# Attention and a mixture of experts on one core: a norm in six chunks, beta added during steps 1 to 3, one scan for all experts, scores s5 ahead of sums o0

## The reference

```
xn  = layernorm(x)
qkv = xn @ w_qkv                      # 16 heads of 8
a   = softmax(causal(q k^T / sqrt(8))) v
t1  = layernorm(a @ w_proj + b_proj + xn) * gamma + beta
p   = softmax(xn @ Wr^T)              # 8 experts
t2  = sum over the two largest p[e] of p[e] * (gelu(xn @ W1[e] + b1[e]) @ W2[e] + b2[e])
out = x + t1 + t2
```

## Time and profile before

| | |
|---|---|
| median of 3 runs | 849.73 us (847.44 to 850.27) |
| the profiled execution | 851.77 us, span 850.0 us |
| granted TensorE clock, mean | 0.958 of full speed |
| busy: PE, DVE, ACT, POOL | 699.9, 692.9, 525.4, 536.0 us |
| share of the chain that ended last | PE 56%, DVE 13%, issue 7%, POOL 7%, DMA 6%, ACT 5%, SP's queue 5% |

### The profile page before, as it was taken

The page is one execution under the profiler, slowest core; times in us unless marked ns, Lnnn a source line. Parts: engine busy times, 40 slices in busy tenths (PEclk is TensorE's granted clock), DMA queues, the critical chain, the costliest instruction groups (busy, mean ns, idle before and its releaser), DMA issues.

```text
span 850.0 us, 24989 instructions
## 1 busy us (share of the span) xinstructions
PE 699.9 (82%) x7877; PEld 518.1 (61%) x7878; DVE 692.9 (82%) x1617; ACT 525.4 (62%) x1039; POOL 536.0 (63%) x575
## 2 busy tenths in 40 slices
PE   1366579999999999999888888868999999999800
PEld 1243346666666666666655555537888889888800
DVE  5778878898999998989889999557788888888744
ACT  4541346565656565656556565537989999999800
POOL 8750456767676776767777777334767676667710
PEclk9999899999999999999999999978999999999955
DMA  8294122232323232232233432202222222222189
GB/s 220 80 400 122 64 84 94 81 111 79 114 77 111 80 111 94 94 98 90 84 127 107 139 125 78 64 7 62 84 85 80 85 88 84 82 82 82 56 266 335
DMA packets 113313, 93.66 MB, mean 110 GB/s; under 512 B 16618, under 2 KB 97650, under 8 KB 113268
## 3 DMA queue, kind: packets, MB, share of 16 engines
q1 hardware_dynamic: 95508, 70.26, 27.0%
q0 software_dynamic: 8704, 18.17, 5.9%
q10 hardware_dynamic: 9056, 4.66, 1.9%
HBM read 43.85 MB, written 48.93 MB: 109 GB/s over the span
## 4 chain that ended last, share of the span: by engine, by line
PE 56%; DVE 13%; issue 7%; POOL 7%; DMA 6%; ACT 5%; SPq 5%; DVEq 0%; ACTq 0%; POOLq 0%
PE wide L1259 10%; PE bank_head L1148 7%; PE wide L1113 5%; PE bank_head L1250 5%; PE bank_maxB L1250 5%; PE bank_maxA L1127 4%; PE bank_maxB L1127 3%; DMA xn_rows<-parts_dram 3%; DMA k_cat<-qk_rows 3%; DVE shift L911 3%; POOL probs L581 3%; PE bank_misc L1173 3%; SPq L478 2%; PE bank_maxB L1131 2%; PE bank_maxA L1131 2%
## 5 line engine op out<-in xcount | busy, mean ns | idle before, releaser
L581 POOL TENSOR_SCALAR_AFFINE_SELECT probs<-probs 128x512 f32<-128x512 f32 (+1 forms) x192 | 158.3, 833 | 103.6 <-ACT probs L653 102.8
L653 ACT ACTIVATE probs<-wide 128x1024 f32<-128x1024 f32 x192 | 188.8, 1018 | 47.3 <-PE wide L1117 24.5
L619 POOL DMA_INDIRECT parts_dram<-o_T,dest x144 | 161.0, 1118 | 74.7 <-issue 48.6
L572 POOL DMA_INDIRECT x_slots<-xn_rows,slot_i x128 | 127.3, 995 | 62.8 <-DVE slot_i L868 31.4
L911 DVE TENSOR_REDUCE shift<-bank_maxA 128x2 f32<-128x512 f32 (+1 forms) x192 | 132.1, 688 | 20.1 <-PE bank_maxA L1131 12.9
L911 DVE TENSOR_REDUCE shift<-bank_maxB 128x2 f32<-128x512 f32 (+1 forms) x192 | 131.5, 685 | 4.9 <-PE bank_maxB L1131 0.8
L687 ACT ACTIVATE probs<-wide,b_all 128x256 f32<-128x256 f32 x288 | 121.4, 478 | 16.8 <-PE wide L1259 10.0
L1148 PE MATMUL bank_head<-probs,v_aug 128*32 128x256 f32 (+1 forms) x2048 | 98.9, 334 | 19.1 <-POOL probs L581 18.9
L1259 PE MATMUL wide<-xgT_raw,xnT 128*128 128x256 f16 x864 | 109.2, 277 | 3.7 <-DVE xgT_raw L1020 3.6
L1003 DVE TENSOR_TENSOR probs<-probs 128x512 f16<-128x512 f32 x144 | 99.7, 692 | 5.5 <-ACT probs L693 1.1
L1127 PE MATMUL bank_maxA<-k_cat,q_diag 128*128 128x128 f16 (+1 forms) x512 | 76.2, 252 | 28.5 <-DVE shift L911 19.5
(11 more groups left out here) (174 smaller groups left out, 1252.4 us busy)
## 6 DMA issues: line engine op xcount, KB each, us to landing
qk_rows<-split SPq DMA_DIRECT2D x32, 512.0 KB, 3.2
x_slots<-fill SPq DMA_DIRECT2D x16, 598.5 KB, 7.6
fill<-x_slots SPq DMA_DIRECT2D x72, 133.0 KB
q_diag<-qk_rows SPq DMA_DIRECT2D x256, 32.0 KB
k_cat<-qk_rows SPq DMA_DIRECT2D x64, 128.0 KB
xn_rows<-parts_dram SPq DMA_DIRECT2D x8, 1024.0 KB, 11.8
x_all<-in_x SPq DMA_DIRECT2D x8, 512.0 KB, 7.6
pieces_f<-in_w SPq DMA_DIRECT2D x8, 512.0 KB, 4.8
```

Source lines behind the costliest of these rows:

```text
L572: pool.indirect_dma_start(out=x_slots, out_offset=bass.IndirectOffsetOnAxis(ap=slot_i[:, t, c:c + 1], axis=0), in_=xn_rows[:, t, :], in_of ...
L581: pool.affine_select(out=part, in_=part, compare_op=ALU.is_ge, fill=0.0, base=0, pattern=[[0, n], [1, P]], channel_multiplier=-1).then_inc ...
L619: pool.indirect_dma_start(out=parts_dram, out_offset=bass.IndirectOffsetOnAxis(ap=dest[:, of, t:t + 1].bitcast(U32), axis=0), in_=y[:, of ...
L653: act.activation(probs[:, u, :], ps[:, :], ACT.Exp, scale=SCALE).then_inc(empty, 1)
```

## The change

- The norm's chunks become six, (0,8), (8,16), (16,24), (24,40), (40,56), (56,64); ScalarE normalises 13 groups and VectorE three. VectorE's low parts of step 0 come after the sixth chunk. The memset of q_diag is cut in two, and router and qkv weights have semaphores of their own.
- Beta is added in four parts after the picks (beside step 1), two at the end of step 2 and two at the end of step 3, on GpSimd.
- The counts per tile come ordered by expert, and one scan over 512 elements, with a 0 in a multiplier at each expert's first tile, does the work of eight. The weights leave `places` and are made by `weights` at the end of step 2 on VectorE.
- Sends begin in step 3 (SEND = FINISH). In even steps from 24 the places are m0, m0, s2 instead of m0, s1, s3.
- In `USES`, s5 comes ahead of o0 and shift.
- ScalarE's high part of a weight piece is made behind `v` instead of at the end of the step.

```diff
-        SEND = SOFT
+        SEND = FINISH
...
-            ("wide0", "s4", SOFT), ("maxB", "m11", MAXIMA), ("head", "o0", SOFT),
-            ("misc", "shift", MAXIMA), ("wide1", "s5", SOFT), ("head", "proj", FINISH),
+            ("wide0", "s4", SOFT), ("maxB", "m11", MAXIMA), ("wide1", "s5", SOFT),
+            ("head", "o0", SOFT), ("misc", "shift", MAXIMA), ("head", "proj", FINISH),
...
-                places = ("m0", "s1", "s3") if (s - TAIL) % 2 == 0 else SEND_AFTER
+                places = ("m0", "m0", "s2") if (s - TAIL) % 2 == 0 else SEND_AFTER
...
-        ACT_GROUPS = 12
+        ACT_GROUPS = 13
...
-        MOMENTS = [(0, 8), (8, 16), (16, 32), (32, 48), (48, 64)]
+        MOMENTS = [(0, 8), (8, 16), (16, 24), (24, 40), (40, 56), (56, 64)]
...
-            pool.memset(q_diag[:, 0, :, :, :], 0.0).then_inc(consts, 1)
             for c, (begin, end) in enumerate(MOMENTS):
+                if c < 2:
+                    pool.memset(q_diag[:, 0, 2 * c:2 * c + 2, :, :], 0.0).then_inc(consts, 1)
...
-            for c in range(BETA_PARTS):
+            def add_beta(c):
                 tiles_ = slice(NT // BETA_PARTS * c, NT // BETA_PARTS * (c + 1))
-                wait_normed(pool, 2 * c + 1)
                 pool.tensor_tensor(x_all[:, tiles_, :], x_all[:, tiles_, :],
...
+            pool.wait_ge(route, ROUTE_PICKED + 1)
+            for c in range(BETA_PARTS // 2):
+                add_beta(c)
...
                 if isinstance(s, int) and s == SEND:
                     pool.wait_ge(slots_filled, 256)
-                    pool.wait_ge(route, ROUTE_DONE)
+                    pool.wait_ge(route, ROUTE_WEIGHTS)
...
                     if what == SUM_AFTER and has(s, FINISH):
                         sums(s)
+                if s in (2, 3):
+                    for c in range(2 * s, 2 * s + 2):
+                        add_beta(c)
                 if has(s, FINISH):
...
-            act.wait_ge(weights_loaded, 96)
+            act.wait_ge(qkv_loaded, 16)
...
+                        for i in pieces(s):
+                            high_piece(i)
...
-                for e in range(E):
-                    V.tensor_tensor_scan(place[:, :, e], ones[:, :], total.rearrange("p (t e) -> p t e", e=E)[:, :, e],
-                                         padded[:, e:e + 1], ALU.mult, ALU.add).then_inc(route, 1)
-                    route_count += 1
-                dve.wait_ge(exp_router, 2)
-                then(V.tensor_reduce(red[:, :], prob[:, :, :], axis=AX.X, op=ALU.add))
+                first_tile_total = total.rearrange("p (e t) -> p e t", e=E)[:, :, 0]
+                then(V.tensor_tensor(first_tile_total, first_tile_total, padded[:, :], ALU.add))
+                dve.wait_ge(consts, 31)
+                then(V.tensor_tensor_scan(place_by_expert[:, :, :].rearrange("p e t -> p (e t)"), goes_on[:, :, :].rearrange("p e t -> p (e t)"), total, 0.0,
+                                          ALU.mult, ALU.add))
...
+            def weights():
+
+                nonlocal route_count
+                dve.wait_ge(exp_router, 2)
+                then(V.tensor_reduce(red[:, :], prob[:, :, :], axis=AX.X, op=ALU.add))
+                V.tensor_scalar(xn_rows[:, :, D + 4], best[:, 0, :], -1.0, float(E), ALU.mult, ALU.add).then_inc(route, 1)
+                route_count += 1
+                then(V.reciprocal(xn_rows[:, :, D], red[:, :]))
+                then(V.scalar_tensor_tensor(out=xn_rows[:, :, D + 2], in0=top[:, 1, :], scalar=-1.0, in1=xn_rows[:, :, D],
+                                            op0=ALU.add, op1=ALU.mult))
...
+                if isinstance(s, int) and s == SOFT:
+                    weights()
...
             moments(4)
             low_group(4)
+            low_group(5)
+            tiles_moments(56, 64)
+            offsets(4)
+            moments(5)
+            low_group(6)
+            step(0, 0)
+            low_group(7)
...
-            dve.wait_ge(offset_ready, BETA_PARTS)
```

More of the change, by code:

```diff
@@ L109, in attention_and_moe @@
         piece = (pieces_f32[:, 0, :], pieces_f32[:, 1, :])
-        others, place, rank, prob = (probs[:, u, 0:NT * E].rearrange("p (t e) -> p t e", e=E) for u in range(4))
+        others, place, rank = (probs[:, u, 0:NT * E].rearrange("p (t e) -> p t e", e=E) for u in range(3))
+        place_by_expert = probs[:, 3, 0:NT * E].rearrange("p (e t) -> p e t", e=E)
+        prob = sb("prob", [P, NT, E])
+        goes_on = probs[:, 5, 512:1024].rearrange("p (e t) -> p e t", e=E)
         is_top16, key16 = (probs[:, 4, NT * E // 2 * u:NT * E // 2 * (u + 1)].bitcast(BF16).rearrange("p (t e) -> p t e", e=E) for u in range(2))
@@ L171, in attention_and_moe @@
         x_loaded = [sem(f"x_loaded{c}") for c in range(2 * CHUNKS)]
+        router_loaded = sem("router_loaded")
+        qkv_loaded = sem("qkv_loaded")
         weights_loaded = sem("weights_loaded")
@@ L382, in attention_and_moe @@
         EXPERTS_PACKED = 16
-        ROUTE_DONE = 38
-        MOMENTS = [(0, 8), (8, 16), (16, 32), (32, 48), (48, 64)]
-        assert NT == 64 and 4 * ACT_GROUPS == MOMENTS[-1][0]
+        ROUTE_DONE = 27
+        ROUTE_WEIGHTS = 31
+        MOMENTS = [(0, 8), (8, 16), (16, 24), (24, 40), (40, 56), (56, 64)]
+        assert NT == 64
         EARLY_AFTER = 4
@@ L653, in exp, with high_piece @@
                 act.activation(probs[:, u, :], ps[:, :], ACT.Exp, scale=SCALE).then_inc(empty, 1)
+            def high_piece(i):
+                act.wait_ge(piece_loaded[i % 2], 16 * (i // 2 + 1))
+                act.activation(part_of(i, 0), piece[i % 2], ACT.Copy).then_inc(piece_high, 1)
             def step(s, par):
@@ L678, in step @@
                         exp(s, int(what[1:]))
-                for i in pieces(s):
-                    act.wait_ge(piece_loaded[i % 2], 16 * (i // 2 + 1))
-                    act.activation(part_of(i, 0), piece[i % 2], ACT.Copy).then_inc(piece_high, 1)
             def hidden(s, par, e, half_):
@@ L953, in last @@
                 dve.wait_ge(rstd2_ready, b * 1 + 1)
+                if isinstance(s, int) and s == LAST:
+                    dve.wait_ge(offset_ready, BETA_PARTS)
                 for t in range(QT):
@@ L1034, in _ @@
             moments(1)
-            tiles_moments(16, 24)
+            tiles_moments(16, 20)
             offsets(1)
-            tiles_moments(24, 32)
+            low_router()
+            tiles_moments(20, 24)
             moments(2)
+            tiles_moments(24, 28)
             low_group(0)
+            offsets(2)
+            tiles_moments(28, 32)
+            low_group(1)
             tiles_moments(32, 40)
-            offsets(2)
-            low_group(1)
-            tiles_moments(40, 48)
             moments(3)
             low_group(2)
-            tiles_moments(48, 56)
+            tiles_moments(40, 48)
             offsets(3)
             low_group(3)
-            step(0, 0)
-            tiles_moments(56, 64)
+            tiles_moments(48, 56)
             moments(4)
             low_group(4)
-            dve.wait_ge(rstd_ready, 5)
-            cols = slice(*MOMENTS[4])
-            V.tensor_scalar(mean[:, cols], mean[:, cols], 0.5, None, ALU.mult).then_inc(prep, 1)
-            prep_count += 1
-            dve.wait_ge(prep, prep_count)
+            low_group(5)
[5 more added lines that the diff above has]
+            low_group(7)
+            dve.wait_ge(rstd_ready, 6)
+            half_of_mean(ACT_GROUPS)
             for g in range(ACT_GROUPS, GROUPS):
                 normalise_group(g)
-                low_group(g - ACT_GROUPS + 5)
-            for g in range(GROUPS - ACT_GROUPS + 5, GROUPS):
+                low_group(g - ACT_GROUPS + 8)
+            for g in range(GROUPS - ACT_GROUPS + 8, GROUPS):
                 low_group(g)
             picks()
-            dve.wait_ge(offset_ready, BETA_PARTS)
             steps(dve, step, after=((), (places,)), first_tile=lambda: tile(0, 0, None))
@@ L1096, in count_picks @@
                 pe.wait_ge(route, ROUTE_PICKED + 1)
-                for n_, counting in enumerate((after16, ones16)):
+                for n_, (counting, order_) in enumerate(((after16, "p t e -> p (t e)"), (ones16, "p t e -> p e t"))):
                     for c in range(2):
-                        last = M(wide[1][:, 512 * n_:512 * (n_ + 1)], counting[:, :], pick16[:, c, :, :].rearrange("p t e -> p (t e)"),
+                        last = M(wide[1][:, 512 * n_:512 * (n_ + 1)], counting[:, :], pick16[:, c, :, :].rearrange(order_),
                                  start=(c == 0), stop=(c == 1))
```

42 lines of the change are left out of this document (27 added, 15 removed).

## The result

The changed kernel takes 860.05 us (median of four, 855.81 to 861.56) against 849.25 for the kernel before in the same comparison; the ratio is 1.0129, 95% interval 1.0088 to 1.0169. The prediction was 854.2, range 841 to 860, with "slower" as the likeliest sign: the sign was right, the size was not. The profiled execution took 861.56 us with a span of 859.5, so the spans differ by +9.5 us where the prediction's sum was +4.5.

What follows compares the result with a forecast made beforehand. The attention loop takes most time, bound by dependency cycles with TensorE and VectorE nearly full. Terms -10.8 + 0.45 - 0.7 + 3.8 + 0.45 + 8.6 + 2.7 = +4.5 us on the 849.73 median gave 854.2 us, range 841 to 860.

Steps and rivals of the forecast that it cites:

- The start: Up to o0 of step 2: 10.8 us gained, bound by SyncE's queue, less 0.45 for s5's new place.
- One scan: Places on VectorE: one scan of 512 takes 1.4 us instead of 2.02 for eight; hidden, counted as nothing.
- Step 2 to 3: Beta 4, 5 at step 2's end and no sends there: -0.7 us, s5's price included; from -2 to +2.
- The end of step 3: Beta 6, 7 on GpSimd block VectorE's packing of the experts: +3.8 us; s5's order adds 0.45 to step 4.
- s5 ahead of o0: Attention loop: s5's matmuls delay o0, copy and proj, no new wait: +0.45 us a step, 8.6 over 19 steps.
- rival A: Attention loop: s5's new order is free or gains up to 0.25 us a step; 840.6 or 836 us; chance 0.22.
- Steps 24 on: Late loop steps with sends, transfers and weight pieces: +2.7 us in sum, from -6 to +9.
- order: s5's new order in the late steps: +0.45 us in each of nine steps, 4.1 in all.
- places: Third tile's sends moved earlier in late even steps: -1.2 us in each of three, -0.8 for step 24.
- high parts: Late steps: ScalarE converts a weight piece earlier and waits for its load: 0.5 us in six steps, +3.0.
- The signs to look for: Expected in a later profile: step 14.4 us, no o1 wait, 0.35 at proj, store near 73, packing 8 us long.

Runs made afterwards that it cites:

- run 5: Changed kernel with GpSimd's last two beta parts, at the end of step 3, waiting until VectorE has packed the experts: 858.69 us, ratio 1.0102.
- run 2: Kernel before with one edit only, s5 ahead of o0 and shift in USES: 867.84 us, ratio 1.0201.
- run 7: Kernel before with s5 ahead of o0 and shift, and only half of s3's exponentials made from step 3 on: 866.07 us, ratio 1.0172.
- run 8: Changed kernel with both tiles of a step sent behind m0, none behind the mask of s2: 861.00 us, ratio 1.0129.
- run 3: Changed kernel with GpSimd masking s5 only after all of VectorE's `last` of the same step: 858.82 us, ratio 1.0090.
- run 6: Changed kernel with bias loads on ScalarE's queue and the two weight pieces on SyncE's in step 3: 855.27 us, ratio 1.0054.
- run 9: Kernel before with s5 ahead of o0 and shift, half of s3's exponentials left out, both tiles sent behind m0: 858.45 us, ratio 1.0095.
- run 1: Changed kernel with only the order of USES put back, s5 again behind o0 and shift: 843.28 us, ratio 0.9902.
- run 12: Changed kernel with old s5 order, last two betas behind the packing, bias loads and weight pieces off SyncE's queue before step 1's store: 833.01 us, ratio 0.9788.

## Why the prediction was right and wrong

**The start, -10.35, measured -8.6.** Right in mechanism; the five traces with this start give 6.4 to 8.6 us. VectorE's groups of four took 1.11 and 1.12 us, and the picks began at 48.89 (predicted 51), step 2's maxima on TensorE at 80.37 (80.4). Two errors cancelled on the way there: the store was issued at 70.57 instead of 73.3, but its rows landed 5.7 us later instead of some 2.8. The first reduction then began at 81.87, a us later than predicted, because TensorE ran the first scores near the lower of its two levels, 1.2 GHz. The same busy sums, with the granted clock third from the end:

```profile
69.00:80.30 11.30, 0.08 (x1) 0.00 (x0) 6.75 (x15) 0.00 (x0) 0.00 (x0) 0.55 0.52 164
80.37:84.50 4.13, 4.03 (x22) 2.67 (x22) 1.73 (x3) 0.60 (x1) 0.00 (x0) 0.58 0.11 29
```

TensorE was idle from 69 to 80.3 with a granted clock of 0.55, and worked at 0.58 until 84.5.

**One scan.** The scan of 512 took 1.22 us (predicted 1.4); as said, it lay under the queue. Step 2 to 3, -0.7, measured -0.1: small and not followed up.

**The end of step 3, +3.8 and 0.45, measured +4.5**, and 4.1 by run 5. The loss was predicted in place and size, but not by the instructions named: not sixteen, each held up, but one, ahead of them, held up for both betas together. It has a single input in SBUF, which the earlier trace rows had already shown for the halving. The Trainium skill, "SBUF — State Buffer", section "Who interferes with whom", lists `tensor_scalar` among the instructions that can take the shared pair in a two-port mode; the trace agrees (3.61 us against 0.17). Its exception for reductions was not put to the test, since the reduction came after the betas.

**The step that failed: "s5 ahead of o0 ... +0.45 us a step", 19 x 0.45 = 8.6; it measured 16.1.** The cycle that was named is the right one, and rival A, a free or gaining s5, falls by run 2. Two readings of that step were wrong.

- "The scores s5 need wide1, freed when the exponential of s3 ends, which is just as m11 ends: no new wait." The two ends are equal: in the step shown m11's last matmul ends at 248.71 and the exponential at 248.69. But TensorE does not wait for a matmul's end to begin the next. In run 7, with the bank free, s5 starts 0.11 us behind the start of m11's last matmul (253.84 and 253.95); in the changed kernel it starts 0.30 behind it (248.44 and 248.74). On a cycle with nothing to spare that is a wait in every step: 0.20 by run 7, where the meeting below is absent.
- What the earlier s5 does to VectorE and GpSimd was not looked at. Everything behind s5 shifts against everything ahead of it: `last` against the second send, by hundredths of a us. In 16 of 19 steps of the changed kernel's trace it falls on the wrong side, and VectorE's `last` becomes the longest cycle: 0.16 a step by run 8 and 0.18 by run 3, but only 0.09 against runs 5 and 6. That it fell so in this execution is luck.

Sum. In the kernel before, the order alone costs 0.68 (run 2): 0.27 of it went with half of s3's exponential and the sends together (run 9; 0.20 the wait for wide1, 0.07 not placed), and 0.42 is left. That is what s5's own matmuls push o0 back behind m11 (0.85 - 0.42 = 0.43, run 7), and what the prediction had put at 0.45. In the changed kernel 0.10 of the 0.85 is not from the order (run 1, open, and as large as the spread between traces), and 0.74 is: the same parts, and 0.09 to 0.18 for the meeting. They don't add exactly, since two cycles of nearly the same length hide one another. What was put at nothing is the wait for wide1, and `last` against the send was not in the sum at all.

**Steps 24 on, +2.7, measured -1.3.** All three terms had the right sign: order +3.55 (152.67 - 149.12; predicted 4.1), places -6.5 (4.4), high parts +1.65 (3.0). The send places were undervalued.

**The signs to look for** held but two: no wait at o1, 0.40 at proj, the store behind the pieces (at 70.57, not near 73), ScalarE's piece copies waiting for their load, though only 2.1 us in four. The step was 14.8 instead of 14.4, and the packing itself stayed at 4.5 us and started late.

## What to carry to other kernels

In a loop in which TensorE is 98% busy and VectorE 91%, "they end at the same time" is not a price of nothing: ask when the next instruction could have started, 0.11 us behind the start of the one ahead here, write that down to a hundredth and charge the difference in every step. When an instruction is moved, look at what it shifts against what on the engines that share something, not only at its own cycle; a start that falls 0.04 us behind another's can cost more than what the move saved. And test parts of a change one by one: this one held a loss of 17 us beside a gain of 7, and with the order put back, the betas moved and the queue freed it is 2.1% faster than the kernel before. Before a step's length is explained, look at a second trace of the same code: the meeting that looked like the changed kernel's own was nearly absent in two others.

## What the runs showed of the hardware

- A few hundredths of a us decide whether VectorE is held up beside an indirect send. The second of two y (scalar_tensor_tensor of 128x128 with two inputs in SBUF) took 0.34, and 0.72 to 0.86 in each of the 45 steps in which the send had started no later than the first y. That an indirect send does this at all was new to me.
- x_all, one such instruction, took 0.34 us at the least (run 8), 0.68 to 0.74 in most steps, and 1.76 where it began inside the second of three GpSimd masks back to back (it ended 0.15 us behind the third). Where it began inside the first, 0.19 us behind its start, it took 0.72 (run 2).
- A TENSOR_SCALAR of 128x2 with one input took 3.61 us beside two GpSimd additions of 128x1024, while two batch-norm statistics from 109.89 and two aggregates from 110.48, beside the same additions, took 0.49 and 0.25.
- A store of 512 KB issued directly behind sixteen fills of 598 KB had its rows read 11.7 us after its issue (run 6), against 3.3 to landing in the median of its 32 stores.
- The same 8 KB bias load held the queue that issued it for 6.65 us on SyncE (changed kernel), and for 9.70 and 12.52 us on ScalarE (runs 6 and 12), whose own instructions had to wait.
